# Six of fifteen levels as ScalarE signs, diagonals from ScalarE, first compares moved forward

## What is computed

```python
blocks = w.reshape(-1, 64)
scalers_1 = max(abs(blocks), axis=1)
scaled = blocks / scalers_1
idx = argmin(abs(scaled - NF4), axis=-1)         # the nearest of 16 levels
weight = NF4[idx] * dequantised(scalers_1)       # the scalers themselves quantised to 8 bits
h = silu(x @ w1.T) * (x @ w2.T);  out = h @ w3.T
```

## Time and profile before

| | us |
|---|---|
| median of 3 runs | 1588.51 (1588.39 to 1589.93) |
| profiled execution | 1587.9 |
| its span | 1586.1 |
| TensorE busy | 1477.4 (93%) |
| VectorE busy | 919.3 (58%) |
| ScalarE busy | 570.4 (36%) |
| GpSimd busy | 255.1 (16%) |
| granted clock, mean | 0.981 |

### The profile page before, as it was taken

One profiled execution on the slowest core, in us unless ns is written; L12 is line 12 of the kernel. 1 busy time (PEld: TensorE's weight loads), 2 busy tenths in 40 slices (PEclk: granted clock), 3 DMA queues, 4 the chain that ended last, 5 costly groups with the idle time before them and its releaser, 6 DMA issues.

```text
span 1586.1 us, 21810 instructions
## 1 busy us (share of the span) xinstructions
PE 1477.4 (93%) x8366; PEld 863.7 (54%) x8366; DVE 919.3 (58%) x1724; ACT 570.4 (36%) x905; POOL 255.1 (16%) x463
## 2 busy tenths in 40 slices
PE   4899899999998999988999998999989999999998
PEld 1344333333333333325677776787767767767776
DVE  9887777778777777864646446303455014571053
ACT  4567266566655566662511111111111211111110
POOL 5023062342624335100000000000000000000000
PEclk9899799999999999999999999999999999999999
DMA  5012223243433333214634011000020000200000
GB/s 169 5 31 84 69 76 108 95 132 96 129 113 122 114 109 111 82 42 177 214 100 126 1 59 49 1 0 1 28 81 1 0 0 28 80 1 1 0 1 27
DMA packets 65917, 105.56 MB, mean 67 GB/s; under 512 B 12527, under 2 KB 37623, under 8 KB 65799
## 3 DMA queue, kind: packets, MB, share of 16 engines
q1 hardware_dynamic: 65335, 103.77, 20.5%
q10 hardware_dynamic: 480, 0.39, 0.1%
HBM read 82.40 MB, written 21.35 MB: 65 GB/s over the span
## 4 chain that ended last, share of the span: by engine, by line
PE 68%; DVE 14%; DMA 7%; ACT 5%; issue 2%; SPq 2%; ACTq 1%; POOL 0%; DVEq 0%; POOLq 0%
PE double L1519 11%; PE double L1533 9%; PE double L1543 7%; PE pV L845 6%; PE level L364 4%; PE level L826 4%; PE double L1582 4%; PE double L1575 3%; PE double L1559 3%; PE double L1550 3%; PE level L835 3%; DMA xres<-in_x 3%; PE pM L780 3%; DVE nmx L1146 3%; PE pM L786 2%
## 5 line engine op out<-in xcount | busy, mean ns | idle before, releaser
L1146 DVE TENSOR_REDUCE nmx<-level 128x1 f32<-128x512 f32 x512 | 322.1, 682 | 62.9 <-PE level L826 62.2
L921 ACT ACTIVATE prob<-level 128x512 f32<-128x512 f32 x512 | 269.4, 602 | 138.5 <-PE level L835 137.3
L835 PE MATMUL level<-Qs,Ks 108*128 108x512 bf16 x512 | 194.7, 383 | 22.1 <-ACT prob L921 21.9
L826 PE MATMUL level<-Ks,Qs 105*128 105x512 bf16 x512 | 201.2, 395 | 8.1 <-DVE nmx L1146 6.1
L1620 ACT ACTIVATE th<-double 128x512 f32<-128x512 f32 x96 | 53.9, 561 | 405.6 <-PE double L1519 209.6
L1519 PE MATMUL double<-x_parts,f0w 128*128 128x256 f16 x1408 | 157.1, 274 | 4.3 <-PEq L501 1.6
L1519 PE MATMUL double<-x_parts,f1w 128*128 128x256 f16 x1408 | 155.2, 273 | 0.0
L364 PE MATMUL level<-prob,x_parts 128*128 128x512 bf16 x540 | 122.5, 384 | 32.8 <-ACT prob L316 14.7
L1519 PEld LDWEIGHTS double<-x_parts,f0w 128*128 128x128 bf16 x1408 | 138.1, 98 | 24.0 <-DVE hid L1717 2.3
L1519 PEld LDWEIGHTS double<-x_parts,f1w 128*128 128x128 bf16 x1408 | 137.7, 98 | 19.2 <-issue 2.3
L1663 POOL TENSOR_TENSOR rstd<-meanvar,halfpow 128x2 f32<-128x2 f32 x22 | 15.2, 689 | 777.9 <-DVE meanvar L1683 777.9
(11 more groups left out here) (174 smaller groups left out, 1878.5 us busy)
## 6 DMA issues: line engine op xcount, KB each, us to landing
scr_q<-qp SPq DMA_DIRECT2D x16, 384.0 KB, 9.1
scr_k<-qp SPq DMA_DIRECT2D x16, 384.0 KB, 3.4
Qs<-scr_q SPq DMA_DIRECT2D x32, 192.0 KB
Ks<-scr_k SPq DMA_DIRECT2D x32, 192.0 KB
hid<-in_f1w1t SPq DMA_DIRECT2D x8, 704.0 KB, 6.2
hid<-in_f1w2t SPq DMA_DIRECT2D x8, 704.0 KB, 4.1
xin<-in_x SPq DMA_DIRECT2D x8, 512.0 KB, 13.1
cx<-in_ctx SPq DMA_DIRECT2D x8, 512.0 KB, 13.3
```

What stands on the lines that cost most here:

```text
L826: nc.tensor.matmul(pA[n % 3], Qs[0:MAX_ROW, g, j, P * tt:P * (tt + 1)], Ks[0:MAX_ROW, g, j, :], start=True, stop=True).then_inc(s["a_pe"], 1)
L835: nc.tensor.matmul(pB[n % 3], Ks[:, g, j, P * c:P * (c + 1)], Qs[:, g, j, :], start=True, stop=True).then_inc(s["b_pe"], 1)
L921: nc.scalar.activation(prob[:, c, j, :], pB[(64 * b + 16 * g + 4 * c + j) % 3], ACT.Exp).then_inc(s["exp_done"], 1)
L1146: nc.vector.tensor_reduce(nmx[:, g % 2, u // 4, u % 4:u % 4 + 1], pA[(64 * b + 16 * g + u) % 3], AX.X, ALU.max, negate=True).then_inc(s["m ...
```

## The change

Six thresholds go to ScalarE and nine stay with VectorE, the rings become 5 and 6 slots, and `MIX` is written anew, with a compare from position 1 on. The diagonals are made by ScalarE, as 15 copies of the identity with a scale, and behind them ScalarE does one small Sign. The first unit's first six compares now stand ahead of `peaks(1)` and `prepare(1)`, the other three behind them.

```diff
--- before.py
+++ after.py
@@ -122,15 +122,15 @@
     UNITS = 12
     CHUNKS = ((0, 512), (512, 448), (960, 448))
 
-    ON_ACT = (2, 5, 8, 11, 14)
+    ON_ACT = (2, 4, 7, 9, 12, 14)
     ON_DVE = tuple(i for i in range(1, 16) if i not in ON_ACT)
     NA, ND = len(ON_ACT), len(ON_DVE)
-    RING_A, RING_D = 4, 7
+    RING_A, RING_D = 5, 6
     RISE = [None] + [LEVEL[i] - LEVEL[i - 1] for i in range(1, 16)]
     OFFSET = LEVEL[0] + sum(RISE[i] for i in ON_ACT) / 2
 
-    MIX = [("a", 0), ("a", 1), ("d", 0), ("a", 2), ("d", 1), ("d", 2), ("d", 3), ("a", 3), ("d", 4), ("d", 5),
-           ("d", 6), ("a", 4), ("d", 7), ("d", 8), ("d", 9)]
+    MIX = [("a", 0), ("d", 0), ("d", 1), ("a", 1), ("d", 2), ("d", 3), ("a", 2), ("d", 4), ("a", 3), ("d", 5),
+           ("a", 4), ("d", 6), ("d", 7), ("a", 5), ("d", 8)]
     TAKE_AFTER = (1, 3, 4)
 
 
@@ -159,6 +159,7 @@
     wq = keep["x_early"][:].bitcast(BF16)[:, 0:WIDE]
     diag = keep["x_parts"][:].rearrange("p r k t -> p (r k t)").bitcast(BF16).rearrange("p (l c) -> p l c", c=P)
     edge = sb("level_edge", [P, NA], F32)
+    sign_junk = sb("sign_junk", [P, NA], F32)
     peak = sb("block_peak", [P, 3, BPP], F32)
     rpeak = sb("block_peak_inv", [P, 3, BPP], F32)
     rep = sb("block_scale", [P, 3, BPP], BF16)
@@ -304,7 +305,12 @@
             act.wait_ge(turned, sum(t[0] == "turn" for t in sides[:n + 1]))
             nc.scalar.activation(target(job), turned_view(job), ACT.Copy).then_inc(turned_act, 1)
 
+        act.wait_ge(const_b, 1)
+        for i in range(1, 16):
+            x = nc.scalar.activation(diag[:, i, :], keep["identb"][:], ACT.Copy, scale=RISE[i] / 2 if i in ON_ACT else RISE[i])
+        x.then_inc(diag_set, 1)
         act.wait_ge(edge_set, NA)
+        nc.scalar.activation(sign_junk[:], edge[:], ACT.Sign)
         taken = 0
         for u in range(UNITS):
             w, q = u // 4, u % 4
@@ -378,12 +384,6 @@
     def vector(dve):
         step = Chain(dve, chain)
 
-        dve.wait_ge(const_b, 1)
-        for i in range(1, 16):
-            x = nc.vector.tensor_scalar(diag[:, i, :], keep["identb"][:],
-                                        RISE[i] / 2 if i in ON_ACT else RISE[i], None, ALU.mult)
-        x.then_inc(diag_set, 1)
-
         def peaks(n):
             w, lo, hi = PEAKS[n]
             dve.wait_ge(w_in[w] if n else w_first, 16)
@@ -402,9 +402,9 @@
             nc.vector.tensor_scalar(part, part, -1.0, None, ALU.max).then_inc(clipped, 1)
             dve.wait_ge(clipped, u + 1)
 
-        def steps(u):
+        def steps(u, first=0, last=ND):
             w, q = u // 4, u % 4
-            for j in range(ND):
+            for j in range(first, last):
                 n = ND * u + j
                 if n >= RING_D:
                     dve.wait_ge(d_used, n - RING_D + 1)
@@ -459,10 +459,12 @@
 
         peaks(0)
         prepare(0)
-        peaks(1)
         for u in range(UNITS):
             if u >= 2:
                 dequantise(u - 2)
+            if u == 0:
+                steps(0, 0, RING_D)
+                peaks(1)
             if u + 1 < UNITS:
                 prepare(u + 1)
             if u == 1:
@@ -471,7 +473,7 @@
                 scaler_sums(1)
             if u == 4:
                 scalers(1)
-            steps(u)
+            steps(u, 0 if u else RING_D)
             for n in PEAKS_AFTER.get(u, ()):
                 peaks(n)
             if u == 0:
```

## The result

| | before | changed |
|---|---|---|
| median, same chip, 16 runs each | 1591.65 us (1587.49 to 1594.2) | 1596.97 us (1592.01 to 1601.41) |
| ratio to before, 95% interval | | 1.0038 (1.0026 to 1.005) |
| profiled execution, its span | 1587.9, 1586.1 | 1600.14, 1598.4 |
| first row score (end of the weights block) | 177.5 | 184.25 |
| granted clock, mean | 0.981 | 0.973 |

The changed kernel is slower, by 1591.65 x 0.0038 = 6.0 us (4.1 to 8.0). The forecast was +1.8, and the time of 1596.97 lies 2 us above the range. 3.1 us of the distance in time are not the change's: before itself came out at 1591.65 here and not at 1588.51. On the 1588.51 from which the prediction started, the ratio gives 1594.5, inside the range by 0.5 us, but the effect is still three times the forecast one.

What follows compares the result with a forecast made beforehand. VectorE bounds the weights block until unit 4 starts, TensorE after. A VectorE lead of -3.7 us and TensorE costs of +5.5 gave +1.8, 1590.3 us on the median of 1588.51, written as 1590; range 1584 to 1595.

Steps and rivals of the forecast that it cites:

- The part on which the sign hangs: Units 4, 5, 8, 9, 10: another sign delays ScalarE's first-turn copy; TensorE waits 0.8, 0.65, 2.1, 2.75, 0.65 us.
- 3.66 less 2.97: Units 5 and 10: 3.66 us until the first turn is copied, against five levels of 2.97; stall put at 0.65.
- The longer stalls in units 8 and 9 bring TensorE's clock down: Rival, 15%: slow multiplies after those stalls, +1.85 us a fall, two falls +3.7, net +5.5, 1594.0 us.
- It decides somewhere between the stall of 1.39 us ... and the 3.6 us: TensorE's clock falls above some stall length between 1.39 us (no fall seen) and 3.6 us ahead of unit 4.
- The lead at unit 4: VectorE reaches unit 4 ahead by 2.4 + 0 + 0.85 + 0.44 = 3.7 us, from units 0 to 3.
- Unit 3 has no such wait: 0.44: Unit 3: VectorE waits for no ring slot, so one compare less saves its full 0.44 us.
- the six compares: First unit, VectorE beside GpSimd: six compares take 5.5 us, four at 0.84 and two slower; possible 2.6 to 8.2.
- the faster preparation of unit 1: VectorE before unit 0's last three compares: unit 1's product and clipping were put at 3.38 us, as before.
- the +5.5 of the forecast: TensorE from unit 4 on: 0.7 at the handover plus stalls in units 4, 5, 8, 9, 10 cost 5.5 us.
- held constant here: Attention and dense layers behind the weights block, some 1409 us, stay untouched; moving by over 1 us would refute it.
- 3 us more than 5.5: First unit: under an exclusive port lock, two of six compares wait for GpSimd's subtraction; 3 us more, total 1593.
- long subtraction: GpSimd instruction of 2.55 us, expected beside the first unit's six compares.

Runs made afterwards that it cites:

- e2: Kernel before with only six ScalarE signs, rings 5 and 6 and the new order of levels; ratio 1.0032, +5.1 us against before.
- e3: Changed kernel with each first copy of a turn one sign earlier in ScalarE's queue; ratio 0.9989, -1.8 us against before.
- e4: Kernel before with one extra, unused ScalarE sign in each of units 8 and 9; ratio 1.0038, +6.0 us against before.
- e5: Changed kernel with the long waits of units 8 and 9 filled by multiplies with an all-zero diagonal; ratio 1.0030, +4.8 us against before.
- e12: Repeat of the changed kernel with waits filled by multiplies with zeros, on the chip of the changed kernel's rerun; ratio 1.0028, +4.5 us against before.
- the third part: Six ScalarE signs, rings 5 and 6 and the new order of levels, put alone on the kernel before; ratio 1.0032, +5.1 us.
- e9: Kernel before with an extra, unused ScalarE sign of half length (704 columns) in units 8 and 9; ratio 1.0019, +3.0 us against before.
- e11: The changed kernel again, unchanged; ratio 1.0031, +4.9 us against before, weights block's end at 177.09 us.
- look 1: The changed kernel, unchanged, profiled once more; weights block's end at 179.30 us, rest of the span 1413.4 us.
- second look: The kernel before, unchanged, in a further profiled execution; weights block's end at 177.85 us, rest of the span 1413.65 us.

## Why the prediction was wrong

Right, step by step. The first maximum started at 4.35 us (4.5), the first compare at 8.87 (8.9), unit 0 ended at 25.7 (25.5), and unit 1 had the one wait (1.64 us, 1.8 forecast). Unit 2's lead was 3.3 us (3.25). The part on which the sign hangs held to 0.1 us: TensorE waited 0.69, 0.69, 2.09, 2.74 and 0.69 us for the copies in units 4, 5, 8, 9 and 10, where the forecast had 0.8, 0.65, 2.1, 2.75 and 0.65 (its own terms, 3.66 less 2.97, give 0.69). e2, e3 and e4 show that this queue is the cause: put in alone it gives the loss, taken out alone it gives it back.

The step that failed is that the sum put nothing for TensorE's clock behind the longer waits. By terms, in the first execution, where the block came out at +6.75 instead of +1.8:

- **The clock behind the waits, 3.4 us.** "The longer stalls in units 8 and 9 bring TensorE's clock down" had 15%, as a rival outside the sum. It happened there twice: 1.30 + 0.41 for multiplies and turn in unit 8, and 1.69 in unit 9. Of the twelve waits of 2.09 to 2.75 us in six such executions (the changed kernel's four, e2, e4) seven were followed by a fall, at 1.7 us each: 2.0 us per execution on average (1.7 in the changed kernel's four). It should have been a term of the sum with a chance, not a case that is there or not. Its size (1.85 a fall) was nearly right. "It decides somewhere between the stall of 1.39 us ... and the 3.6 us" was not: waits of one length went either way.
- **The lead at unit 4, 1.3 us, which was this execution's chance.** It was 2.4 instead of 3.7: against "Unit 3 has no such wait: 0.44" the clock was low in unit 3, the last compare waited 0.89 us, and the mean came 0.43 us late. The three later executions have no such wait, and over all four unit 4's first compare starts at 78.2 us in the mean, against 82.0 in before's three: a lead of 3.8. So that term holds. Inside it two errors cancelled: the six compares took 6.69 us instead of 5.5, and the faster preparation of unit 1 (20.65 to 23.17, 2.5 us for 3.4) covered most of that.
- The remaining 0.2 to 0.3 us are spread over the hand-overs.

Without falls the four executions would end at 184.25 - 3.4, 177.09, 179.30 and 181.31 - 3.4, in the mean 178.8, against 177.5 of before's three. That is +1.3, where the sum had +1.8: from unit 4 to the block's end it is 100.6 us against 95.5, +5.1 for the +5.5 of the forecast, less the lead of 3.8. So the sum was nearly right, and what it left out is the clock. With the falls the mean is 180.5, +3.0: they account for 1.7 to 2.0 of the 3.1 to 4.2 us between forecast and measured, and for the rest no run shows a cause. The medians of 16 and 12 executions say +6.0 and +4.9, with intervals that reach from 2.7 to 8.0. Whether the missing 2 to 3 us are more falls than in my four executions, or lie in the attention part, isn't settled. The four profiled executions themselves are 4.4 us longer than before's three (1595.8 against 1591.4), 3.0 of it in the block and 1.4 behind it, and these 1.4 hang on the low 1408.6. The rest of the span varied between 1408.6 and 1417.9 us over all executions, though "held constant here" was the forecast. e5 and e12 speak for something beside the falls: +4.8 and +4.5 without any in units 8 and 9 of their traces.

The Trainium skill (SBUF — State Buffer, "SBUF: two separate sides") has the port that VectorE and GpSimd share as an exclusive lock, by which I had estimated 3 us more than 5.5 for the six compares. They took 6.69, 1.1 each. The trace agrees with the lock for the compares: each ended 0.4 us behind the end of a GpSimd instruction, one for one, and 0.4 is about what a compare takes by itself (0.44). The estimate failed by what it put beside them. The "long subtraction" of 2.55 us was long in the kernel before only: it started at 8.75 us there, beside VectorE's product of 8.67 to 10.29, and in the changed kernel the same instruction took 1.30 us. The prediction's own 5.5 took too little as well, for it let only two of the six be slower than 0.84. That it was the port, and nothing else that orders the two engines, no run shows.

For the table load the Trainium skill (ScalarE: Activation LUTs, "What ACT_TABLE_LOAD costs") has a drain of 1.38 us behind it at a change of set. Here, at the first load of the kernel, the trace has none: 1.28 us from 0.74, and the first diagonal at 2.03.

## What to carry to other kernels

Before work is moved to an engine with spare time, find what that engine owes the bounding one in mid-queue, and count the instructions that stand ahead of it: here 1.36 us of sign was 1.36 us of stall, though ScalarE was busy for 36% of the span, and moving one copy by one place undid it. Read the busy share in the stage that changes, too: it was 67% there. Price a stall of the bounding engine also by what its clock may do afterwards, with a chance, and look at several executions before a clock state of one trace enters a sum. Do one part of a bundled change at a time: here the diagonals alone gave 2.9 us, and the third part cost 5.1 us alone and, by the two measurements, 7.8 to 8.9 on top of the others.

## What the hardware showed

TensorE's granted clock fell to half behind waits of 2.09 to 2.75 us in seven of twelve cases, and in e9 behind 2.16; behind waits of 0.7 to 1.5 us it never fell in these units. The same wait of 2.75 us passed without a fall in e2, e11 and look 1, and one of 3.14 us ahead of unit 4 in e11. At the end of the block the clock was at 0.50 in the first execution of before, behind waits of 1.12, 0.58 and 1.12 us close together, and at 1.00 behind the same three in its second look: the length of the wait alone doesn't decide, and short waits are not safe everywhere. Each fall in units 8 and 9 lasted some 3 us, within one group of fifteen multiplies (4.4 to 4.8 us instead of 3.13). Multiplying by zero through the wait went with a clock of 1.00 in both executions. A ScalarE copy of 128x128 with a factor came every 0.21 us, under half of the 0.485 of 128x384. A VectorE compare of 128x1408 beside a row of short GpSimd instructions ended once per GpSimd instruction, every 0.85 or 1.4 us, against 0.44 by itself.
